# A two-layer recurrent block on one core: routing intermediates in PSUM, and another order of the gated multiplies

## The reference

```python
xn = layernorm(x)
s = L0_attn(xn)                      # linear attention, layer norm, Wo
g = silu(L0_ffn(xn))                 # below
x = x + s * g
xn = layernorm(x)
s = L1_attn(xn)                      # a scan, below
g = silu(L1_ffn(xn))                 # 8 experts, the best 2 of a softmax
x = x + s * g

# L0_ffn: 32 experts of width 64, 8 chosen per token, and a shared one
g = x @ expert_gate[e].T;  u = x @ expert_up[e].T
outs[e] = (silu(g) * u) @ expert_down[e].T      # times the token's gate for e

# L1_ffn, the second routing
probs = softmax(x @ gate_w.T + gate_b)          # 8 experts
gate = probs where the rank is below 2, else 0
out = sum_e gate[e] * (relu(x @ w1[e] + b1[e]) @ w2[e] + b2[e])

# L1_attn: 9 levels, d = 1, 2, 4, ... 256
left = x shifted by d tokens;  v = (left + x) @ W, in 4 lanes of 32 channels
att = softmax(left . x over lanes);  z = att @ v
x = left + rms_norm(z) / (1 + lane)
```

## Time and profile before

| | us |
|---|---|
| median of 3 runs | 552.67 (550.68 to 553.13) |
| the profiled execution | 552.49 |
| its span, first to last instruction | 550.7 |
| busy: TensorE, VectorE, GpSimd, ScalarE | 510.7, 461.3, 359.9, 331.1 |

### The profile page before, as it was taken

One profiled execution on the slowest core, in us unless ns is written; L12 is line 12 of the kernel. 1 busy time (PEld: TensorE's weight loads), 2 busy tenths in 40 slices (PEclk: granted clock), 3 DMA queues, 4 the chain that ended last, 5 costly groups with the idle time before them and its releaser, 6 DMA issues.

```text
span 550.7 us, 9020 instructions
## 1 busy us (share of the span) xinstructions
PE 510.7 (93%) x2860; PEld 409.2 (74%) x2860; DVE 461.3 (84%) x871; ACT 331.1 (60%) x934; POOL 359.9 (65%) x325
## 2 busy tenths in 40 slices
PE   3989999999999999669899999999999999999945
PEld 3855776776677676458789879889888988888734
DVE  6955876976895688989988899999999999999886
ACT  3441252254226234447688888898888888888670
POOL 3960010013204375867799999999999999999850
PEclk9997999999999999758899999999999999999887
DMA  7541323323323232001011120111112121101002
GB/s 221 203 154 64 113 82 111 100 87 110 96 96 101 100 103 68 19 24 34 21 57 25 36 58 23 55 39 41 39 39 59 24 54 39 38 23 38 20 2 76
DMA packets 26675, 37.09 MB, mean 67 GB/s; under 512 B 4480, under 2 KB 12296, under 8 KB 26500
## 3 DMA queue, kind: packets, MB, share of 16 engines
q1 hardware_dynamic: 26628, 36.52, 21.4%
HBM read 25.75 MB, written 1.31 MB: 49 GB/s over the span
## 4 chain that ended last, share of the span: by engine, by line
PE 73%; DVE 8%; ACT 6%; POOL 6%; issue 3%; DMA 3%; SPq 0%; POOLq 0%; DVEq 0%; ACTq 0%
PE bank L591 69%; PE bank L594 4%; DMA left_tok<-state_ext 2%; DVE shared L1630 2%; POOL shared L527 2%; POOL shared L535 1%; DVE ln_stats L1289 1%; ACT shared L1185 1%; DVE bank L1604 1%; ACT shared L1163 1%; DVE shared L1305 1%; DMA x<-in_x 1%; POOL shared L514 1%; POOL state_ext L548 0%; POOL xn L456 0%
## 5 line engine op out<-in xcount | busy, mean ns | idle before, releaser
L591 PE MATMUL bank<-w,shared 128*128 128x128 f32 x1024 | 123.9, 280 | 0.1
L591 PE MATMUL bank<-xnT_lo,wgu_hi 128*128 128x512 f32 x264 | 120.4, 456 | 2.7 <-ACT shared L1185 2.6
L591 PEld LDWEIGHTS bank<-w,shared 128*128 128x128 f32 x1024 | 118.1, 194 | 5.6 <-ACT shared L1185 5.5
L591 PE MATMUL bank<-xnT_hi,wgu_lo 128*128 128x512 f32 x264 | 105.6, 400 | 0.0
L591 PE MATMUL bank<-xnT_hi,wgu_hi 128*128 128x512 f32 x264 | 104.6, 396 | 0.0
L527 POOL TENSOR_TENSOR shared<-shared 128x1024 f32<-128x1024 f32 x35 | 83.9, 2396 | 18.6 <-DVE shared L1630 18.6
L1039 ACT ACTIVATE shared<-bank 128x512 f32<-128x512 f32 x68 | 40.7, 598 | 90.1 <-PE bank L591 89.8
L591 PE MATMUL bank<-shared 128*128 128x512 f32 (+3 forms) x280 | 90.1, 444 | 1.1 <-ACT shared L1014 1.1
L1185 ACT ACTIVATE shared<-bank,b 128x512 f32<-128x512 f32 x128 | 83.0, 716 | 1.0 <-PE bank L591 1.0
L1630 DVE TENSOR_TENSOR shared<-shared,bank 128x2048 f32<-128x2048 f32 x36 | 82.0, 2278 | 0.0
L1424 DVE TENSOR_TENSOR shared<-shared,bank 128x512 f32<-128x512 f32 x64 | 43.8, 685 | 29.7 <-PE bank L591 19.0
(11 more groups left out here) (176 smaller groups left out, 807.4 us busy)
## 6 DMA issues: line engine op xcount, KB each, us to landing
shared<-gate_rows SPq DMA_DIRECT2D x122, 128.0 KB, 2.9
w<-in_w SPq DMA_DIRECT2D x8, 256.0 KB, 2.9
shared<-in_w SPq DMA_DIRECT2D x1, 2048.0 KB, 9.2
left_tok<-state_ext SPq DMA_DIRECT2D x16, 128.0 KB
left_tok<-state_ext SPq DMA_DIRECT2D x8, 224.0 KB
left_tok<-state_ext SPq DMA_DIRECT2D x8, 192.0 KB
shared<-in_wd SPq DMA_DIRECT2D x1, 1088.0 KB, 11.7
x<-in_x SPq DMA_DIRECT2D x4, 256.0 KB, 3.7
```

The costliest lines, as they stand in the source:

```text
L591: return nc.tensor.matmul(out, lhsT, rhs, start=start, stop=stop)
```

## The change

Two parts, both about where operands lie.

**Mixture, items 3 to 63.** ScalarE writes silu back into the gate bank, not to SBUF. VectorE's first multiply is then gate bank by the gates' row, its second is that product by the up bank; before, the row was multiplied second, with both inputs in SBUF. The new semaphore `gated_done` counts the first multiply, and `h0_done` still the second. So the gate bank comes free with `gated_done` (before: `silu_done`), and the up bank with `h0_done` (before: `gu_done`). The first multiply waits for the row's transfer and no longer for the up bank. Items 0 to 2 are as before.

**Second routing.** Ranks (`erank`), reciprocals (`lrec`) and probabilities (`probs1`) lie in a bank beside the logits or the scores (`beside`), not in SBUF, and L1545's subtraction reads the logits' copy in the bank, for which it now waits.

```diff
@@ gate_up (TensorE) @@
-                for m, out, free in ((0, bank[G[i % 2]], "silu_done"), (1, bank[U[i % 2]], "gu_done")):
-                    after(pe, s(free), i - 1)
+                for m, out in ((0, bank[G[i % 2]]), (1, bank[U[i % 2]])):
+
+                    if i - 2 < item(RING):
+                        after(pe, s(("silu_done", "gu_done")[m]), i - 1)
+                    elif m == 0:
+                        pe.wait_ge(s("gated_done"), i - 1 - item(RING))
+                    else:
+                        pe.wait_ge(s("h0_done"), i - 1 - item(0))
@@ sum_channels, values (TensorE), left_out (ScalarE): first use of the banks in the scan @@
-                    pe.wait_ge(s("silu_done"), item(B * PAIRS))
+                    pe.wait_ge(s("gated_done"), B * PAIRS - RING)
...
-                    pe.wait_ge(s("gu_done"), item(B * PAIRS))
+                    pe.wait_ge(s("h0_done"), B * PAIRS)
...
-            act.wait_ge(s("silu_done"), item(B * PAIRS))
+            act.wait_ge(s("gated_done"), B * PAIRS - RING)
@@ silu_gate (ScalarE) @@
-                after(act, s("gu_done"), i - 1)
-                a.activation(silu_g[:, i % 2], bank[G[i % 2]][:], ACT.Silu).then_inc(s("silu_done"), 1)
+                if i < item(RING):
+                    after(act, s("gu_done"), i - 1)
+
+                a.activation(silu_g[:, i % 2] if i < item(RING) else bank[G[i % 2]][:], bank[G[i % 2]][:], ACT.Silu).then_inc(s("silu_done"), 1)
@@ routed_hidden (VectorE), n >= RING @@
-                dve.wait_ge(s("u_mm"), i + 1)
-                tt(silu_gu[:, i % 2], silu_g[:, i % 2], bank[U[i % 2]][:], ALU.mult).then_inc(s("gu_done"), 1)
-                dve.wait_ge(s("gu_done"), i + 1)
...
-                tt(h0[:, n % RING], silu_gu[:, i % 2], gate_rows[n % RING] if n >= RING else bank[GB][:], ALU.mult).then_inc(s("h0_done"), 1)
+                dve.wait_ge(s(f"ld_rows{n % RING}"), 32 * (n // RING))
+                tt(silu_gu[:, i % 2], bank[G[i % 2]][:], gate_rows[n % RING], ALU.mult).then_inc(s("gated_done"), 1)
+                dve.wait_ge(s("gated_done"), n - RING + 1)
+                dve.wait_ge(s("u_mm"), i + 1)
+                dve.wait_ge(s("dn_mm"), downs(n - RING))
+                tt(h0[:, n % RING], silu_gu[:, i % 2], bank[U[i % 2]][:], ALU.mult).then_inc(s("h0_done"), 1)
@@ second routing (VectorE) @@
+            def beside(k, at):
+                part = bank[k][:, at:at + 2 * HT * E1 + HT]
+                tiles = [part[:, n * HT * E1:(n + 1) * HT * E1].rearrange("p (t e) -> p t e", t=HT) for n in range(2)]
+                return tiles + [part[:, 2 * HT * E1:]]
+
+            erank, probs1, lrec = zip(beside(AT, HT * E1), beside(Y, 256))
...
-                tt(lsub[:], logits1[:], lmax[:].unsqueeze(2).broadcast_to([P, HT, E1]), ALU.subtract).then_inc(s("lsub_done"), 1)
+                dve.wait_ge(s("log1_cp"), 2 * half + 2)
+                tt(lsub[:], log, lmax[:].unsqueeze(2).broadcast_to([P, HT, E1]), ALU.subtract).then_inc(s("lsub_done"), 1)
...
-                v.tensor_reduce(erank[:], ecmp[:], AX_X, ALU.add).then_inc(s("route1_step"), 1)
+                v.tensor_reduce(erank[half], ecmp[:], AX_X, ALU.add).then_inc(s("route1_step"), 1)
...
-                ts(emask[:], erank[:], 2.0, None, ALU.is_lt).then_inc(s("route1_step"), 1)
+                ts(emask[:], erank[half], 2.0, None, ALU.is_lt).then_inc(s("route1_step"), 1)
...
-                tt(probs1[:], lexp[:], lrec[:].unsqueeze(2).broadcast_to([P, HT, E1]), ALU.mult).then_inc(s("route1_step"), 1)
+                tt(probs1[half], lexp[:], lrec[half].unsqueeze(2).broadcast_to([P, HT, E1]), ALU.mult).then_inc(s("route1_step"), 1)
...
-                tt(gate1[:, tiles], probs1[:], emask[:], ALU.mult).then_inc(s("gate1_done"), 1)
+                tt(gate1[:, tiles], probs1[half], emask[:], ALU.mult).then_inc(s("gate1_done"), 1)
```

More of the change, by code:

```diff
@@ L278, in build @@
             "woc_done gram_mm gram_cp q_mm q_cp route0_step parts_done g0T_mm g0T_cp "
[L279 removed]
+            "g_mm u_mm gb_mm st_gates ld_rows0 ld_rows1 ld_rows2 silu_done gu_done gated_done h0_done dn_mm y0_silu y0T_mm sg_done x1_done "
             "m1_mm m1_done st_mm st_done head_mul state_done stT_mm stT_cp so_mm so_cp at_mm at_cp at_stat at_var_done "
@@ L1422, in routed_hidden @@
                 dve.wait_ge(s("silu_done"), i + 1)
-                dve.wait_ge(s("u_mm"), i + 1)
-                tt(silu_gu[:, i % 2], silu_g[:, i % 2], bank[U[i % 2]][:], ALU.mult).then_inc(s("gu_done"), 1)
-                dve.wait_ge(s("gu_done"), i + 1)
-                if n < RING:
-                    dve.wait_ge(s("gb_mm"), n + 1)
-                else:
-                    dve.wait_ge(s(f"ld_rows{n % RING}"), 32 * (n // RING))
-                if n >= RING:
-                    dve.wait_ge(s("dn_mm"), downs(n - RING))
-                tt(h0[:, n % RING], silu_gu[:, i % 2], gate_rows[n % RING] if n >= RING else bank[GB][:], ALU.mult).then_inc(s("h0_done"), 1)
+                if n < RING:
+                    dve.wait_ge(s("u_mm"), i + 1)
+                    tt(silu_gu[:, i % 2], silu_g[:, i % 2], bank[U[i % 2]][:], ALU.mult).then_inc(s("gu_done"), 1)
+                    dve.wait_ge(s("gu_done"), i + 1)
+                    dve.wait_ge(s("gb_mm"), n + 1)
+                    tt(h0[:, n % RING], silu_gu[:, i % 2], bank[GB][:], ALU.mult).then_inc(s("h0_done"), 1)
+                    return
+                dve.wait_ge(s(f"ld_rows{n % RING}"), 32 * (n // RING))
+                tt(silu_gu[:, i % 2], bank[G[i % 2]][:], gate_rows[n % RING], ALU.mult).then_inc(s("gated_done"), 1)
+                dve.wait_ge(s("gated_done"), n - RING + 1)
+                dve.wait_ge(s("u_mm"), i + 1)
+                dve.wait_ge(s("dn_mm"), downs(n - RING))
+                tt(h0[:, n % RING], silu_gu[:, i % 2], bank[U[i % 2]][:], ALU.mult).then_inc(s("h0_done"), 1)
             def key_values_out(b):
```

6 lines of the change are left out of this document (1 added, 5 removed).

## The result

The change is faster by more than predicted: 544.38 us median (542.93 to 547.16, 4 runs) against 552.44 (550.68 to 553.13), ratio 0.9863 [0.9837, 0.9890]. The prediction was 548.7, range 546.0 to 551.6. A later repeat on another occasion gave 544.12 against 552.55, ratio 0.9859 [0.9823, 0.9896]. So 8.1 to 8.4 us went where 3.9 were forecast.

A forecast was written before the change was run, and what follows sets the result against it. GpSimd's unbroken rounds, fixed by the start of slot 10's `halve_mix`, were taken to bound the end. 1.22 us at the turn plus 2.67 us by slot 4 made 3.9 us, giving 548.7 us, range 546.0 to 551.6.

The forecast's parts named there:

- The sum of 3.9 us: Whole kernel: 1.22 + 2.67 us saved, carried through slots 4, 6, 8 and 10 to the end.
- the second term: Second routing, slots 2 to 4: 3.0 us saved on VectorE, of which 2.67 us count by slot 4.
- what bounds: Scan: GpSimd's unbroken rounds of 8.06 us from slot 10 on; the start of slot 10's `halve_mix` fixes the end.
- the collisions: VectorE ops with both inputs in SBUF and GpSimd ops hold each other up; one bank input avoids it.
- the first term: Turn after the mixture: GpSimd's ops up to `sum_inputs(0, 0)` lose their collisions, 1.22 us, bounds 0.8 to 1.4.
- no price in the mixture: Mixture: both multiplies priced at 0.69 us, effect counted 0 because TensorE sets the pace and waits for neither product.
- The rival of a late gate bank: Mixture: first multiply waits for the row transfer, gate bank comes free too late; slower, 555.6 us, chance 0.07.
- the rival of waits that do not go: Long ops come from something other than two SBUF inputs; nothing moves, 552.6 us, chance 0.06.
- the rival that slot 3's gain is given back: ScalarE's relus or TensorE's expert matmuls keep slot 4 where it was; 551.4 us, chance 0.17.
- L1545 (0.77) ... counts 0: Second routing: reading the bank saves about 0.4 us, counted 0 because VectorE then waits for ScalarE's square.
- Undisturbed its hop is ... 16.96 us for two slots: Scan: loop through the shift transfer of about 6 us, limiting slot 4 to 273.67 us.
- transfer loop weaker: Scan: GpSimd runs back to back from slot 3, slot 10 at 321.7 us; 545.9 us, chance 0.11.

The follow-up runs named there:

- shift_only: The kernel before with one edit, L1545's subtraction reading its logits from the bank after a wait for the copy: 550.43 us, ratio 0.9957.
- before_again: The kernel before, the same code measured once more: 552.60 us, ratio 1.0001.
- shift_kept: The change with the subtraction of the row maximum put back to its SBUF input: 545.71 us, ratio 0.9871.
- routing_only: The kernel before with only the second routing's edits, the mixture as before: 545.65 us, ratio 0.9872.
- mixture_only: The kernel before with only the mixture's edits, the routing as before: 550.28 us, ratio 0.9959.
- The fillings: The change with unread matmuls added in one of TensorE's two longest waits at the turn (546.11 us) or in both (545.28 us).

## Why the prediction was wrong, step by step

The sum of 3.9 us fell short in three places above all: L1545 counted 0 where it is worth 1.4 us, the second term was 2.67 where it measured 3.3 to 3.7, and nothing was counted for the course of TensorE's clock, to which an estimate gives the rest.

**Right: what bounds.** GpSimd goes back to back from slot 10 to slot 32 in every kernel, 177.33 to 177.63 us for 22 slots, and what is won ahead of slot 10 is kept until slot 32.

**Right: the collisions.** An op with two SBUF inputs was the long one, and with one of them in a bank it never is. The Trainium skill, "SBUF — State Buffer", section "Who interferes with whom", says that such a VectorE op contends with a GpSimd op that reads SBUF and that one with a single SBUF input does not, outside the modes that use both ports, which it says a tensor_scalar can enter. The runs agree: 2.11 us against 0.22 for the same 128x64 subtraction. L1567, a tensor_scalar with one input, was long as well while that lay in SBUF (1.89 us) and takes 0.22 from the bank, so two SBUF inputs are not the whole of the condition.

**Right: the first term.** 1.22 us predicted, 1.4 measured (23.7 against 22.3 in the turn): L459 0.36, L478 0.45, L511 0.45, and 0.12 in the L453 group, which I had not counted. In the very first pair it was 1.83, since four transposes at 228 us ran before the clock fell (0.67 us) in the change and behind it (1.12) in the kernel before; that part is luck.

**Right: no price in the mixture.** The first multiply from a bank takes 0.691 us and the second 0.686. From 42 to 212 us TensorE's matmuls wait 1.5 us in all, in both kernels, each time for ScalarE and never for VectorE, and the begin of the turn (214.55 and 215.53 us in the change, 214.87 and 215.31 before) shows no delay clear of its spread. The Trainium skill ("VectorE: DVE Perf Modes", the TRN2 errata) has 120 cycles as the fixed part from PSUM against 58 from SBUF; that difference is not seen, with 0.686 to 0.691 us for one input in a bank and 0.692 for none. The rival of a late gate bank, the rival of waits that do not go, and the rival that slot 3's gain is given back all fell.

**Wrong, first: "L1545 (0.77) ... counts 0".** In the execution that I read the step holds, but that execution had the late course. There TensorE's 22 matmuls took 6.34 us, ScalarE's relus, its copy and then its square came late behind them, and VectorE waited for the square. The chain of work that ended last runs this way, and L1545 took 0.77 us only because it was issued late beside slot 1's `halve_mix`. The wait in the kernel before:

```profile
254.82 0.70 DVE L1619 TENSOR_REDUCE z_ms<-shared 128x16 f32<-128x528 f32 x1 [0.51 <-ACT shared L1163]
```

With the early course the cover is gone. The same op takes 2.11 us, the comparisons, `products(2)` and `scores(2)` follow it without a gap, L1619 waits for nothing, and VectorE's queue sets slot 2. The edit is worth 1.4 us then. In the late course nothing shows a gain from it: the 0.30 us between 18.91 and 18.61 lie in three of TensorE's matmuls, since the clock came back sooner (start, us, what; before, then the change):

```profile
251.25 1.00 PE bank L591 x3
```

```profile
250.06 0.71 PE bank L588 x3
```

The unprofiled executions agree. The four of shift_only with a mean granted clock of 0.954 or 0.955, that of before's first profile, took 551.94 to 552.57 us, and the eight such executions of the kernel before beside them 551.88 to 552.79. The step that failed is the cover, taken from one course of the clock as if it were there in all.

**Wrong, second: "Undisturbed its hop is ... 16.96 us for two slots".** I took the average from slot 4 to slot 10 and used it from slot 2 to slot 4. That hop was 16.48 us (8.41 + 8.07), GpSimd's round and 0.30 of waiting. The wait for a transfer is a property of one level, distance 4, whose 124 partitions move on a quarter of the engines; it holds for the `halve_mix` of slots 7 to 10 alone. Splitting that transfer removes it whole. Slot 5, which waited too in the kernel before (8.75 us after slot 4), did so for a TensorE that had stood still: it was busy 2.99 of the 5 us from 265 to 270, and 5.00 in the change, and the chain to slot 5 holds 40 of its matmuls from 271.62 to 278.00 and no transfer. So the second term, 2.67 us predicted, measured 3.3 to 3.7. Its input, 3.0 us saved in the second half, was well sized: 11.6 us from slot 2 to slot 3 became 8.41, so 3.2. The rival "transfer loop weaker", 545.9, had the mechanism nearly right: back to back up to slot 6, and then the loop after all.

**What is left, by an estimate.** The stretches give 1.4 + 1.4 + 3.5 = 6.3 us with an early clock in both kernels. The medians say 8.1 to 8.4. The prediction had no term for the course of the clock, and the other 2 us can be laid to it. Of the 23 executions of the kernel before that ran beside its repeat, 12 have a mean granted clock of 0.954 or 0.955, like its first profile (552.49 us: late course, end 44.74), and 7 have 0.967 or 0.968, like before_again (553.20 us: early course, but end 46.32). The commonest of the change is 0.970, with 544.1 to 544.4 us in four of ten executions, and no profile caught it. The nearest is that of shift_kept, at 0.969. With the repeat's 16.90 us put in for its slots 0-2 its span is 542.5, so 544.3 us, as these four took. Against before's first profile that is 8.2 us: 0.3 at the begin of the turn, 1.9 in the turn, 2.0 in slots 0-2, 3.7 in 2-10, and 0.3 behind. By this estimate the typical execution of the change has the early course with an end near 44.6, where before's has the late course or the long end. In the same way routing_only is 6.3 us below before's first profile by its stretches, for 6.8 or 6.9 by the medians, and mixture_only 2.8 for 2.2 or 2.3.

**Open.** That the executions at 0.970 took this course isn't shown, since only profiled executions show it, and neither is why the change's usual course is another one than that of the kernel before: whether the edits bring it about or it falls so by chance. An end of 43.2 us stands in 3 of the 10 kernels with the whole of the routing's edits or all but L1545's and in none of the other 4, but single executions do not settle it. The fillings, made to take the clock out, did not keep it up reliably.

## What to carry to other kernels

Price a VectorE op that may collide not by its length in one profile but by how much of a GpSimd op can lie ahead of it, and look at what binds there when the clock is at its other level. Before a loop's period is used as a limit, look whether each hop really waits, and on what: here the transfers of one level were the slow ones, and splitting them, or taking the square ahead of their copy, freed 1.9 us. A gain seen in a stretch is to be followed to the end of the span, where a spread of 3 us between executions can cover it.
